# An attention block on one NeuronCore: query and key split in PSUM by TensorE, bias rows as three bf16 rows, sums turned once a batch

## The chip, the cores and the metric

The kernel runs on one NeuronCore of a Trainium2 chip; the other seven are not used. The metric is the device time of one execution in microseconds, the median over runs. Engines: TensorE (PE) multiplies into PSUM, VectorE (DVE), ScalarE (ACT) and GpSimd (POOL) compute, SyncE (SP) issues all DMAs. In this kernel only VectorE and ScalarE read PSUM.

## The reference, cut to what matters

```python
def _layernorm(t, gamma, beta):                      # over the last axis
    return (t - mean) * rsqrt(var + 1e-05) * gamma + beta
xn = (x - mean) / sqrt(var + 1e-05)                  # x is (32, 256, 128), f32
qkv = (xn @ Wqkv.T + bqkv).reshape(B, N, 3, H, D).transpose(2, 0, 3, 1, 4)   # H = 16, D = 8
q = _layernorm(q, q_gamma, q_beta)
k = _layernorm(k, k_gamma, k_beta)
aw = softmax(einsum('bhnd,bhmd->bhnm', q, k) / sqrt(D))
kth = top_k(aw, 12)[0][..., -1:]                     # topk = int(256 * 0.05)
aws = aw * (aw >= kth)
aws = aws / (aws.sum(-1, keepdims=True) + 1e-08)
o_s = einsum('bhnm,bhmd->bhnd', aws, v)
qf, kf = softmax(q), softmax(k)                      # over the 8 channels of a head
kv = einsum('bhnd,bhne->bhde', kf, v)
z = einsum('bhnd,bhd->bhn', qf, kf.sum(axis=2))
o_l = einsum('bhnd,bhde->bhne', qf, kv) / (z[..., None] + 1e-06)
a = sigmoid(alpha)                                   # one per head
o = a * o_s + (1.0 - a) * o_l
attn = o @ Wproj.T + bproj
idx = argmax(log_softmax(logits) + gumbel(u))        # one of 8 operators
y = x + attn + xn @ W[idx] + b[idx]
```

## The kernel before, in words

The 32 batches are 32 iterations `it`, unrolled by four in a hardware loop, with some iterations written out at either end. An iteration is a pass over eight *slots* `u_`, one for each *unit*; a unit is two heads, and for each of them two tiles of 128 queries by 256 keys, four tiles (`TILES`) in all. Each engine runs its own queue in the order in which `body` is written for it, and waits only on semaphores; nothing reorders the work across slots. Work is staged: in one slot each engine serves different units and even different batches.

The main line of unit g: TensorE multiplies its scores one slot ahead (`scores`, L797) into `score_ps`; VectorE takes the 8 largest of each tile (`top`, L503); GpSimd subtracts the maximum (`drop`, L363); ScalarE makes the exponentials `e` (L705) and `e8` (L710); one slot later VectorE strikes the 8 largest out (`rest`, L510) and takes the next 8 (`next`, L516), whose fourth is the threshold; GpSimd (three tiles, L389) and ScalarE (one tile, L718) mark what is `below` it; TensorE transposes `e` and adds -2^40 where `below` is set (`turn`, L814, L815, 16 matmuls a slot, into `turn_ps`); ScalarE's Relu makes `kept` of it (L666); every second slot TensorE multiplies four heads' `kept` by the values `v_aug`, which have a column of ones (`product`, L831, into the bank `pv_ps`), and ScalarE copies that to `oT` (L727).

Once a batch, around this:

- The sums of the four quads of `oT` are transposed back by TensorE (`sums`, L843, into `pv_ps`), for query tile 0 in slot 5 and for tile 1 in slot 7. VectorE adds `den` (L551), takes its reciprocal (L556) and writes `o_sparse` (L559), inside slots 5 and 7, behind its first two `rest`.
- The linear part: q and k of the next batch come out of the product L891 (slot 7, with a bias by a matmul of one row of ones with one row `b_row`, L892), pass ScalarE (`qk_sq`, `qk_raw`) and GpSimd (`qk_a`, `qk_b`, `qkn`), and `d_sub`; `q_exp` and `k_exp` are made by ScalarE in slot 4. In the next iteration TensorE multiplies `kv` (slot 1, L905, L907), transposes `q_exp` (slot 4, L943), ScalarE copies `qfT` (L733), TensorE multiplies both (slot 5, L869), and VectorE makes `lin_z` and `lin` (slot 5, L531, L534). 
- The exact split: `qkn` is transposed by TensorE (slot 3, L930) into the bank `work_ps`. ScalarE copies it to `qkT` in f32 (L686) and to bf16 `part[0]` (L689). GpSimd subtracts (`leave`, L352) to `residue`, ScalarE casts it to `part[1]` (slot 4, L738), once more for `part[2]` (slot 5). SyncE writes every part to DRAM in slots and reads them back as `q_slots` and `k_slots` for the scores of the next batch.
- The value product L880 with its bias L881 (slot 6), copied to `v_aug` (L693).
- The output: `o_sparse` and `lin` are transposed and added (slot 1, L862, L863), copied to `osT` (L672), and multiplied in slot 2, four products for each of two tiles (L918 the residual, L919 the chosen operator, L920 the bias, L921 the projection), copied in slot 3 to `out_sb` (L680) and stored.

All of these but the sums go through the one bank `work_ps`, one after the other, and every step waits for the copy of the last. TensorE's queue in a slot is: turn, product (even slots), sums (5 and 7), `early`, scores for the next unit, `late`.

## Time and profile before

| | |
|---|---|
| median of 3 runs | 1337.95 us (1335.01 to 1338.44) |
| the profiled execution | 1329.16 us, its span 1327.4 us |
| VectorE busy | 1212.3 us, 91% |
| ScalarE busy | 1135.2 us, 86% |
| GpSimd busy | 1092.6 us, 82% |
| TensorE matmul busy | 1051.5 us, 79% |
| DMA | 83.42 MB, 63 GB/s |

The times are those of one execution; "busy" leaves out semaphores, branches and DMA issue. Matmul records overlap, so a row's mean is a latency and not the distance from one to the next. A wait in the profile is idle time of an engine just before an instruction, with what released it. In rows of the timeline the first number is the start in us from the span's start, the second the duration.

### The profile page before, as it was taken

What the parts mean: (1) busy time and instruction counts of PE and PEld (TensorE: products, weight loads), DVE (VectorE), ACT (ScalarE), POOL (GpSimd) and SP (SyncE); (2) the same over time, 40 slices, a digit from 0 to 9 for tenths busy, and PEclk for the clock granted to TensorE, in tenths of its full rate; (3) what the DMA queues carried; (4) which work ended last, traced back from release to release, by engine and by line L of the source; (5) the groups of instructions that cost most, each with busy time, mean ns of one, the idle gap of its engine ahead of it and who ended that gap; (6) DMA issues with size and microseconds to landing.
All of it is one profiled execution on the core that took longest, in us unless ns stands there. A gap on an engine that the chain in (4) does not pass through costs nothing.

```text
span 1327.4 us, 39880 instructions
## 1 busy us (share of the span) xinstructions
PE 1051.5 (79%) x9156; PEld 718.5 (54%) x9156; DVE 1212.3 (91%) x4660; ACT 1135.2 (86%) x3946; POOL 1092.6 (82%) x1618
## 2 busy tenths in 40 slices
PE   3578887878787888887888887788878888887887
PEld 1345555555555555555555555555555555555555
DVE  5789999999899998999989999899989999999994
ACT  3588998998899897998888989788988889998984
POOL 4588888988789887889878889788888888889973
PEclk9979999998899998998989989889998889899998
DMA  2212221222222122221112222112221122221220
GB/s 57 68 45 73 76 77 43 60 65 65 79 77 70 36 64 65 77 77 52 56 53 75 77 77 60 46 53 77 77 79 34 58 65 77 76 77 37 61 58 13
DMA packets 165196, 83.42 MB, mean 63 GB/s; under 512 B 7747, under 2 KB 164933, under 8 KB 164934
## 3 DMA queue, kind: packets, MB, share of 16 engines
q1 hardware_dynamic: 164934, 80.54, 21.1%
q8 instruction: 89, 1.46, 0.5%
q14 instruction: 173, 1.42, 0.4%
HBM read 42.77 MB, written 37.75 MB: 61 GB/s over the span
## 4 chain that ended last, share of the span: by engine, by line
PE 34%; issue 21%; ACT 17%; POOL 13%; DVE 13%; DVEq 1%; POOLq 1%; ACTq 0%; DMA 0%; SPq 0%
PE turn_ps L814 9%; ACT e L705 9%; POOL below L389 8%; DVE rest L510 6%; PE turn_ps L815 4%; DVE top L503 4%; PE work_ps L892 3%; PE work_ps L891 3%; PE pv_ps L831 3%; DVE next L516 3%; PE score_ps L797 2%; PE pv_ps L843 2%; ACT xn L756 2%; PE work_ps L921 2%; ACT below L718 1%
## 5 line engine op out<-in xcount | busy, mean ns | idle before, releaser
L389 POOL TENSOR_SCALAR below<-e,next 128x256 bf16<-128x256 f32 x768 | 695.8, 921 | 0.0
L705 ACT ACTIVATE e<-score_ps,drop 128x256 f32<-128x256 f32 x1024 | 475.4, 492 | 76.1 <-POOL drop L363 75.6
L814 PE MATMUL turn_ps<-ident,e 128*128 128x128 f32 x2048 | 432.8, 304 | 29.1 <-issue 14.5
L510 DVE MATCH_REPLACE8 rest<-e 128x256 f32<-128x256 f32 x1024 | 413.1, 406 | 0.9 <-issue 0.9
L516 DVE MAX8 next<-rest 128x8 f32<-128x256 f32 x1024 | 410.5, 411 | 3.3 <-issue 1.8
L815 PE MATMUL turn_ps<-minus_huge,below 128*128 128x128 bf16 x2048 | 406.4, 234 | 0.0
L503 DVE MAX8 top<-score_ps 128x8 f32<-128x256 f32 x1024 | 360.2, 413 | 37.3 <-PE score_ps L797 19.8
L814 PEld LDWEIGHTS turn_ps<-ident,e 128*128 128x128 f32 x2048 | 314.4, 154 | 97.9 <-issue 31.5
L666 ACT ACTIVATE kept<-turn_ps 128x512 f32<-128x512 f32 x512 | 292.2, 624 | 67.0 <-PE turn_ps L815 62.6
L815 PEld LDWEIGHTS turn_ps<-minus_huge,below 128*128 128x128 bf16 x2048 | 234.7, 115 | 0.0
L705 ACT ACTIVATION_READ_ACCUMULATOR e<-score_ps,drop 128x1 f32 x1024 | 229.3, 224 | 0.0
L363 POOL TENSOR_TENSOR drop<-top 128x36 f32<-128x36 f32 x256 | 62.6, 245 | 133.8 <-DVE top L503 132.6
L831 PE MATMUL pv_ps<-kept,v_aug 128*32 128x256 f32 x2048 | 141.5, 395 | 1.1 <-ACT kept L666 0.7
L718 ACT ACTIVATE below<-e,next 128x256 bf16<-128x256 f32 x256 | 137.0, 535 | 0.2 <-DVE next L516 0.2
L797 PE MATMUL score_ps<-k_slots,q_slots 64*128 64x256 bf16 x1024 | 104.8, 283 | 12.0 <-ACT e L705 10.1
L510 DVE MATCH_VALUE_LOAD rest<-e 128x8 f32 x1024 | 73.2, 71 | 15.0 <-ACT e L710 13.0
L831 PEld LDWEIGHTS pv_ps<-kept,v_aug 128*32 128x32 f32 x2048 | 54.5, 111 | 46.2 <-issue 24.4
L843 PE MATMUL pv_ps<-ident,oT 128*128 128x128 f32 x256 | 49.6, 326 | 36.8 <-ACT oT L727 35.5
L797 PEld LDWEIGHTS score_ps<-k_slots,q_slots 64*128 64x128 bf16 x1024 | 30.7, 95 | 85.8 <-issue 76.6
L710 ACT ACTIVATE e<-drop 128x32 f32<-128x32 f32 x256 | 66.3, 259 | 0.0
L352 POOL TENSOR_TENSOR residue<-qkT,part 128x512 f32<-128x512 f32 x32 | 37.2, 1162 | 32.2 <-ACT part L689 31.9
L843 PEld LDWEIGHTS pv_ps<-ident,oT 128*128 128x128 f32 x256 | 33.7, 168 | 51.0 <-ACT oT L727 49.1
(141 smaller groups left out, 1529.7 us busy)
## 6 DMA issues: line engine op xcount, KB each, us to landing
part_slots<-part SPq DMA_DIRECT2D x128, 192.0 KB, 2.3
q_slots<-part_slots SPq DMA_DIRECT2D x64, 256.0 KB, 3.4
...
```

The costliest lines, as they stand in the source:

```text
L389: nc.gpsimd.tensor_scalar(below[:, r, t, :], e[:, r, t, :], next8[:, r, t, TOPK - 9:TOPK - 8], None, ALU.is_lt).then_inc(s["below_pool"], 1)
L503: nc.vector.max(top[:, q, t, 1:9], score_ps[:, q, t // 2, t % 2, :]).then_inc(s["top_ready"], 1)
L510: nc.vector.match_replace(rest[:, t, :], e8[:, (u_ - 1) % 2, t, :], e[:, (u_ - 1) % RING, t, :], REMOVED).then_inc(s["rest_ready"], 1)
L516: nc.vector.max(next8[:, (u_ - 1) % RING, t, :], rest[:, t, :]).then_inc(s["next_ready"], 1)
L666: nc.scalar.activation(kept[:, u_ % 4, hh], turn_ps[:, hh], ACT.Relu).then_inc(s["turn_copied"], 1)
L705: nc.scalar.activation(e[:, u_ % RING, t, :], score_ps[:, u_ % 2, t // 2, t % 2, :], ACT.Exp, bias=drop[:, u_ % 2, t, 0:1], accum_out=z[:, ...
L718: nc.scalar.activation(below[:, r, t, :], e[:, r, t, :], ACT.Relu, scale=-1.0, bias=next8[:, r, t, TOPK - 9:TOPK - 8]).then_inc(s["below_a ...
L797: last = mm(score_ps[:, v_ % 2, hh, nt, :], q_slots[rows, side, v_, nt * P:(nt + 1) * P], k_slots[rows, side, v_, :], start=True, stop=True)
L814: mm(dst, e[:, r, t, keys], ident[:], start=True, stop=False, is_transpose=True)
L815: last = mm(dst, below[:, r, t, keys], minus_huge[:], start=False, stop=True)
L831: last = mm(pv_ps[32 * j:32 * (j + 1), 0:N], v_aug[:, side, mc, 4 * q + j, :], kept[:, v_ % 4, j % 2, mc, :], start=(mc == 0), stop=(mc == ...
L843: last = nc.tensor.transpose(pv_ps[:, q * P:(q + 1) * P], oT[:, nxt, q, t * P:(t + 1) * P], ident[:])
```

## The change

1. **The split in PSUM.** `qkT`, `residue` and GpSimd's `leave` are gone. ScalarE casts `part[0]` from `work_ps`. TensorE then multiplies `part[p]` by `minus_one` (minus the identity, bf16) into the same bank without clearing it (`remainder`), for p = 0 late in slot 4 and for p = 1 early in slot 5; ScalarE casts `part[1]` and `part[2]` from `work_ps`, in the places where it cast them from `residue`. For that the four transposes of `qkn` are one accumulation group.
2. **Bias rows.** Each bias row is split at the start into three bf16 rows (`in_parts`, on VectorE), and a bias is added by one bf16 matmul with a contraction of three rows (`ones3`, `bias3`) in place of an f32 one with one row.
3. **The sums once a batch.** All eight transposes stand in slot 5, behind the scores. They use the matrix `gather` in place of the identity, which packs four heads' 9 used columns next to each other, so that the sums of both tiles fit the bank. VectorE's `den`, reciprocal and `o_sparse` run once, over both tiles, in slot 5.
4. **Other slots and banks.** `q_exp` is transposed early in slot 0 and copied there at the slot's end; the linear product moves from slot 5 to the end of slot 2, VectorE's `lin_z` and `lin` from slot 5 to slot 3. The transposes of `o_sparse` and `lin`, and the output's products, go to `pv_ps` in place of `work_ps`; the output moves from the end of slot 2 to slot 3, ahead of the scores.

TensorE, slot 5, before: the end of the turn, and what follows up to the scores of unit 6. `oT` are the copied sums, `part` the bf16 part.

```order
L815 MATMUL turn_ps<-minus_huge,below 128x128
L814 MATMUL turn_ps<-ident,e 128x128
L815 MATMUL turn_ps<-minus_huge,below 128x128
L843 MATMUL pv_ps<-ident,oT 128x128 x4
L869 MATMUL work_ps<-kv,qfT 128x144 x2
L73 ISA
L797 MATMUL score_ps<-k_slots,q_slots 128x256 x4
L805 REGISTER_ALU
```

And in the changed kernel, where `gather` stands for the identity:

```order
L834 MATMUL turn_ps<-minus_huge,below 128x128
L833 MATMUL turn_ps<-ident,e 128x128
L834 MATMUL turn_ps<-minus_huge,below 128x128
L871 REGISTER_ALU
L872 MATMUL work_ps<-part,minus_one 128x512
L73 ISA
L816 MATMUL score_ps<-k_slots,q_slots 128x256 x4
L865 MATMUL pv_ps<-gather,oT 128x128 x8
L824 REGISTER_ALU
```

The sums went from ahead of the scores to behind them, four became eight, the linear product left, and the remainder stands ahead of the scores.

TensorE, slot 7, before: the end of the turn, the sums of tile 1 and the query and key product of the batch after the next, up to the scores of the next batch's first unit.

```order
L814 MATMUL turn_ps<-ident,e 128x128
L815 MATMUL turn_ps<-minus_huge,below 128x128
L843 MATMUL pv_ps<-ident,oT 128x128 x4
L885 REGISTER_ALU
L891 MATMUL work_ps<-w_qk,xnT 128x256
L892 MATMUL work_ps<-b_row,ones_row 128x256
L891 MATMUL work_ps<-w_qk,xnT 128x256
L892 MATMUL work_ps<-b_row,ones_row 128x256
L789 REGISTER_ALU
L73 ISA
L797 MATMUL score_ps<-k_slots,q_slots 128x256 x4
```

In the changed kernel:

```order
L833 MATMUL turn_ps<-ident,e 128x128
L834 MATMUL turn_ps<-minus_huge,below 128x128
L924 REGISTER_ALU
L931 MATMUL work_ps<-w_qk,xnT 128x256
L932 MATMUL work_ps<-bias,ones 128x256
L931 MATMUL work_ps<-w_qk,xnT 128x256
L932 MATMUL work_ps<-bias,ones 128x256
L808 REGISTER_ALU
L73 ISA
L816 MATMUL score_ps<-k_slots,q_slots 128x256 x4
```

The sums are gone and the bias is taken from `bias` by `ones`, which are `bias3` and `ones3`.

TensorE, from the scores in slot 2 to the start of the next turn, before:

```order
L797 MATMUL score_ps<-k_slots,q_slots 128x256 x4
L915 REGISTER_ALU
L918 MATMUL work_ps<-x_res,ident 128x128
L919 MATMUL work_ps<-w_sel,xnT 128x128
L920 MATMUL work_ps<-b_out,ones_row 128x128
L921 MATMUL work_ps<-w_proj,osT 128x128
L918 MATMUL work_ps<-x_res,ident 128x128
L919 MATMUL work_ps<-w_sel,xnT 128x128
L920 MATMUL work_ps<-b_out,ones_row 128x128
L921 MATMUL work_ps<-w_proj,osT 128x128
L805 REGISTER_ALU
```

In the changed kernel, first the same place, and then slot 3 from the turn's end to the scores for unit 4:

```order
L816 MATMUL score_ps<-k_slots,q_slots 128x256 x4
L950 MATMUL work_ps<-kv,qfT 128x144 x2
L824 REGISTER_ALU
```

```order
L834 MATMUL turn_ps<-minus_huge,below 128x128
L901 REGISTER_ALU
L904 MATMUL pv_ps<-x_res,ident 128x128
L905 MATMUL pv_ps<-w_sel,xnT 128x128
L906 MATMUL pv_ps<-bias,ones 128x128
L907 MATMUL pv_ps<-w_proj,osT 128x128
L904 MATMUL pv_ps<-x_res,ident 128x128
L905 MATMUL pv_ps<-w_sel,xnT 128x128
L906 MATMUL pv_ps<-bias,ones 128x128
L907 MATMUL pv_ps<-w_proj,osT 128x128
L73 ISA
L816 MATMUL score_ps<-k_slots,q_slots 128x256 x4
```

The linear product stands where the output stood, and the output stands between the turn of slot 3 and the scores, in the bank `pv_ps`.

The diff, cut (left out: GpSimd's setup of the constants `minus_one`, `gather` and `ones3`, buffers and loads that go from one partition to three, and waits that follow from the moves):

```diff
-if u_ == 4 and exists(it + 1):
-    leave(it, 0)
-if u_ == 5 and exists(it + 1):
-    leave(it, 1)
...
+def in_parts(row, cols):
+
+    p0, p1 = bias_part[:, 0, cols], bias_part[:, 1, cols]
+    r1, r2, total = bias_rest[:, 0, cols], bias_rest[:, 1, cols], bias_sum[:, cols]
+    own = [ident[0:PARTS, p:p + 1] for p in range(PARTS)]
+    setup(nc.vector.tensor_copy(p0, row))
+    setup(nc.vector.tensor_tensor(r1, row, p0, ALU.subtract))
+    setup(nc.vector.tensor_copy(p1, r1))
+    setup(nc.vector.tensor_tensor(r2, r1, p1, ALU.subtract))
+    setup(nc.vector.tensor_scalar(total, p0, own[0], None, ALU.mult))
+    setup(nc.vector.scalar_tensor_tensor(out=total, in0=p1, scalar=own[1], in1=total, op0=ALU.mult,
+                                         op1=ALU.add))
+    return nc.vector.scalar_tensor_tensor(out=bias3[:, cols], in0=r2, scalar=own[2], in1=total,
+                                          op0=ALU.mult, op1=ALU.add)
...
-if u_ == 5 and 3 <= k <= 5 and exists(it):
+if u_ == 3 and k in (1, 3) and exists(it):
     w = work_ps[:, 0:NT * H * VA].rearrange("p (t h e) -> p t h e", t=NT, e=VA)
-    if k == 3:
+    if k == 1:
...
-if u_ in (5, 7) and 1 <= k <= 4 and exists(it - 1):
-    t = (u_ - 5) // 2
-    w = pv_ps[:].rearrange("p (h e) -> p h e", e=VW)
-    n = 2 * (NT * (it - 1) + t)
+if u_ == 5 and 1 <= k <= 4 and exists(it - 1):
+    w = pv_ps[:, 0:NT * H * VA].rearrange("p (g e) -> p g e", e=VA)
+    n = 2 * (it - 1)
     if k == 1:
-        dve.wait_ge(s["w_turn"], NT * (it - 1) + t + 1)
...
 if u_ == 4 and exists(it + 1):
     act.wait_ge(s["w_qkT"], it + 2)
-    wait(act, s["residue_ready"], 2 * (it + 1))
-    nc.scalar.copy(qkT[:], work_ps[:].rearrange("p (a n) -> p a n", a=2)).then_inc(
-        s["qkT_copied"], 1)
     wait(act, s["slots_written"], 16 * 2 * PARTS * (it + 1))
     nc.scalar.copy(part[:, 0], work_ps[:].rearrange("p (a n) -> p a n", a=2)).then_inc(
         s["part_ready"], 1)
...
-if u_ == 4 and exists(it):
+if u_ == 0 and exists(it):
     act.wait_ge(s["w_qfT"], it + 1)
+    wait(act, s["w_lin"], it)
     nc.scalar.copy(qfT[:], work_ps[:, 0:N]).then_inc(s["qfT_copied"], 1)
 if u_ in (4, 5) and exists(it + 1):
     p = u_ - 3
-    act.wait_ge(s["residue_ready"], 2 * (it + 1) + p)
-    nc.scalar.copy(part[:, p], residue[:, p - 1]).then_inc(s["part_ready"], 1)
+    act.wait_ge(s["w_rest"], 2 * (it + 1) + p)
+    nc.scalar.copy(part[:, p], work_ps[:].rearrange("p (a n) -> p a n", a=2)).then_inc(
+        s["part_ready"], 1)
...
+def sums():
+
+    pe.wait_ge(s["pv_copied"], QUADS * it)
+    for t in range(NT):
+        for q in range(QUADS):
+            at = (t * QUADS + q) * 4 * VA
+            last = nc.tensor.transpose(pv_ps[:, at:at + P], oT[:, nxt, q, t * P:(t + 1) * P], gather[:])
...
+def remainder(p):
+
+    pe.wait_ge(s["part_ready"], PARTS * (it + 1) + p + 1)
+    mm(work_ps[:], minus_one[:], part[:, p].rearrange("p a n -> p (a n)"), start=False,
+       stop=True, skip_group_check=True).then_inc(s["w_rest"], 1)
...
+    if u_ == 0 and exists(it):
+
+        pe.wait_ge(s["dexp_ready"], 2 * it + 1)
         if exists(it + 1):
             pe.wait_ge(s["raw_ready"], it + 2)
...
+if u_ == 3 and exists(it - 2):
+
+    pe.wait_ge(s["osT_copied"], it - 1)
+    pe.wait_ge(s["pv_copied"], QUADS * it - 1 if exists(it - 1) else QUADS * B)
+    pe.wait_ge(s["setup_v"], 7)
+    pe.wait_ge(s["res_loaded"], 16 * (it - 1))
     for t in range(NT):
-        last = mm(work_ps[:, t * H * VA:(t + 1) * H * VA], qfT[:, t * P:(t + 1) * P],
-                  kv[:].rearrange("p h e -> p (h e)"), start=True, stop=True)
-    last.then_inc(s["w_lin"], 1)
+        dst = pv_ps[:, t * C:(t + 1) * C]
+        mm(dst, ident[:], x_res[:, t, :], start=True, stop=False)
+        mm(dst, xnT[:, (xr - 2) % XRING, t * P:(t + 1) * P], w_sel[:], start=False, stop=False)
+        mm(dst, ones3[:], bias3[:, 3 * C:4 * C], start=False, stop=False)
+        last = mm(dst, osT[:, t * P:(t + 1) * P], w_proj[:], start=False, stop=True)
+    last.then_inc(s["w_out"], 1)
+if u_ == 5 and exists(it + 1):
+
+    remainder(1)
...
+    pe.wait_ge(s["part_ready"], PARTS * (it + 2))
     for t in range(NT):
         dst = work_ps[:, t * C:(t + 1) * C]
         mm(dst, xnT[:, (xr + 1) % XRING, t * P:(t + 1) * P], w_v[:], start=True, stop=False)
-        last = mm(dst, ones_row[:], b_row[:, 2 * C:3 * C], start=False, stop=True)
+        last = mm(dst, ones3[:], bias3[:, 2 * C:3 * C], start=False, stop=True)
...
-if u_ == 2 and exists(it - 2):
...
+if u_ == 2 and exists(it):
...
+        last = mm(work_ps[:, t * H * VA:(t + 1) * H * VA], qfT[:, t * P:(t + 1) * P],
+                  kv[:].rearrange("p h e -> p (h e)"), start=True, stop=True)
+    last.then_inc(s["w_lin"], 1)
 if u_ == 3 and exists(it + 1):
...
+    wait(pe, s["lin_ready"], it + 1)
...
+if u_ == 4 and exists(it + 1):
+
+    remainder(0)
...
-if u_ in (5, 7) and exists(it - 1):
-    sums(u_)
 early(u_)
 if exists(it if u_ < UNITS - 1 else it + 1):
     scores(u_)
+if u_ == 5 and exists(it - 1):
+    sums()
 late(u_)
```

## Rows read from the trace of the kernel before

**Rows 1.** The page, busy time of each engine, share of the span, instructions.

```profile
PE 1051.5 (79%) x9156; PEld 718.5 (54%) x9156; DVE 1212.3 (91%) x4660; ACT 1135.2 (86%) x3946; POOL 1092.6 (82%) x1618
```

**Rows 2.** Line 524, once a batch: durations, first and last start in us.

```profile
L524 DVE TENSOR_TENSOR kv<-work_ps,own_head x32: 288/295/298, 49.9 to 1279.1; 128x144 f32<-128x144 f32 x32
```

**Rows 3.** VectorE's waits, 85 to 1240 us: us in total, times, longest.

```profile
DVE den L551 <- PE pv_ps L843: 25.5, 42, 1.0
DVE top L503 <- issue: 16.5, 5, 3.7
DVE rest L510 <- ACT e L710: 10.5, 17, 0.9
DVE top L503 <- PE score_ps L797: 7.7, 17, 0.7
```

**Rows 4.** VectorE by line: busy us, mean ns | idle before, releaser.

```profile
L559 DVE TENSOR_TENSOR o_sparse<-pv_ps,den 128x128 f32<-128x128 f32 x64 | 17.2, 269 | 0.1
...
L556 DVE RECIPROCAL den<-den 128x16 f32<-128x16 f32 x64 | 14.9, 233 | 0.1
...
L534 DVE TENSOR_TENSOR lin<-work_ps,lin_z 128x256 f32<-128x256 f32 x32 | 12.9, 403 | 0.0
L531 DVE RECIPROCAL lin_z<-work_ps 128x32 f32<-128x32 f32 x32 | 11.0, 345 | 0.0
L551 DVE SCALAR_TENSOR_TENSOR den<-z,pv_ps 128x16 f32<-128x16 f32 x64 | 10.7, 167 | 36.0 <-PE pv_ps L843 35.7
```

**Rows 5.** Timeline, slots 4 and 5 of one batch, from four engines.

```profile
650.70 1.40 DVE L503 MAX8 top<-score_ps 128x8 f32<-128x256 f32 x4
...
652.31 0.63 ACT L686 COPY qkT<-work_ps 128x512 f32<-128x512 f32 x1
652.77 0.65 ACT L689 CAST part<-work_ps 128x512 bf16<-128x512 f32 x1
653.31 0.50 ACT L705 ACTIVATE e<-score_ps,drop 128x256 f32<-128x256 f32 x1
...
655.63 0.40 ACT L727 COPY oT<-pv_ps 128x256 f32<-128x256 f32 x1
...
656.09 0.66 PE L843 MATMUL pv_ps<-ident,oT 128*128 128x128 f32 x4 [0.74 <-ACT oT L727]
656.58 0.66 PE L869 MATMUL work_ps<-kv,qfT 128*128 128x144 f32 x4
657.17 0.40 PE L797 MATMUL score_ps<-k_slots,q_slots 64*128 64x256 bf16 x4
...
657.01 0.16 DVE L551 SCALAR_TENSOR_TENSOR den<-z,pv_ps 128x16 f32<-128x16 f32 x1
657.08 0.42 DVE L516 MAX8 next<-rest 128x8 f32<-128x256 f32 x1
```

**Rows 6.** Timeline, slots 2 and 3 of the same batch.

```profile
644.07 0.48 PE L918 MATMUL work_ps<-x_res,ident 128*128 128x128 f32 x2 [1.54 <-issue]
...
646.40 0.49 PE L921 MATMUL work_ps<-w_proj,osT 128*128 128x128 f32 x2
646.41 0.38 ACT L727 COPY oT<-pv_ps 128x256 f32<-128x256 f32 x1
...
648.78 0.37 ACT L680 COPY out_sb<-work_ps 128x256 f32<-128x256 f32 x1
```

**Rows 7.** By line, TensorE's f32 bias and GpSimd's subtraction, as in Rows 4.

```profile
L892 PE MATMUL work_ps<-b_row,ones_row 1*128 1x256 f32 x128 | 48.1, 457 | 0.0
...
L352 POOL TENSOR_TENSOR residue<-qkT,part 128x512 f32<-128x512 f32 x32 | 37.2, 1162 | 32.2 <-ACT part L689 31.9
```

**Rows 8.** TensorE in two turns, slots 5 and 7: us, busy (x), granted clock, DMA.

```profile
653.77:655.35 1.58, 1.58 (x18) 1.00 0.57 166
664.55:667.33 2.78, 2.78 (x18) 0.50 0.54 160
```

**Rows 9.** Timeline, VectorE's first maxima.

```profile
40.33 1.76 DVE L503 MAX8 top<-score_ps 128x8 f32<-128x256 f32 x5 [8.77 <-PE score_ps L797]
```

166 lines of the change are left out of this document (74 added, 92 removed).

## The prediction

> **What bounds the kernel now.** I read the busy shares first. VectorE leads with 91%, ScalarE, GpSimd and TensorE follow at 86, 82 and 79% [rows 1]: four engines that are all nearly full, so the question is which of them sets the pace and how often it stands still. One batch is 1229.2 / 31 = 39.65 us, from the first and last start of an operation that runs once a batch [rows 2]. In the unit loop VectorE has nearly no gap: its waits between 85 and 1240 us, which are 29.1 batches, add up to 43.7 us in the three lines that the change can touch, and 16.5 us in five long "issue" gaps of over 3 us, one at each turn of the hardware loop [rows 3]. The last have no engine behind them, so I leave them as they are. So VectorE sets the pace, and a batch is some 37.6 us of its own work, 0.57 us of loop turns and 43.7 / 29.1 = 1.50 us of waits for others: 25.5 us for the turned sums (`den` <- `pv_ps`), 10.5 us for the exponentials of the unit before (`rest` <- `e`), 7.7 us for scores [rows 3]. Whatever the change does on the other engines counts only through these waits, through VectorE's own instructions, or through a new wait on VectorE.
>
> **Part by part, per batch.** Slot u is pass u of the unit loop.
>
> *VectorE's own work.* Two sets of `den`, reciprocal and `o_sparse` (167 + 233 + 269 ns) become one with twice the elements. The nearest rows of that size are the reciprocal of 32 elements, 345 ns, and the product over 256, 403 ns; `den` of 32 elements I put at 180 ns, 167 plus the little that 16 elements add [rows 4]. That is 1.34 us against 0.93 us by durations, 0.4 us less. But these instructions overlap their neighbours: `den` starts at 657.01 and the MAX8 behind it at 657.08, where `den` lasts 0.16 us [rows 5]. An instruction thus costs some 0.08 us less than its duration, and three fewer of them save 0.41 - 0.24 = 0.17 us, which I take; the bounds are 0.1 and 0.4.
>
> *The sums of slot 7.* The wait of slot 7 (up to 1.0 us [rows 3]) has no instruction left to wait. Four transposes leave TensorE's queue there, and the query and key product loses its f32 bias matmuls, 457 ns each and two per 256 columns [rows 7], for one bf16 pass over the same columns. 128 columns of bf16 with their load take about 0.1 us (the turn's 16 matmuls, half of them bf16, in 1.58 us [rows 8]), so 256 take 0.1 to 0.2 us. The scores for the next batch stand behind that product, so they come over 1 us earlier, and the wait for scores (7.7 us, the longest 0.7) should go too.
>
> *The linear part and the output.* The linear part's product moves from slot 5 to slot 2, the output's four products per tile from slot 2 to slot 3, ahead of the scores for unit 4. Until now TensorE spends 644.07 to 646.89 on the output, and only then turns unit -1, which ScalarE needs before the exponentials of slot 3 [rows 6]. Now two small products stand there. The output must wait for ScalarE's copy of `pv_ps` (646.41 + 0.38 = 646.8 [rows 6]). It took 2.8 us; with bf16 bias it takes 2.2, so it ends at 649.0, and `out_sb`, which was copied at 648.78, is copied at 649.1: ScalarE's exponentials of slot 3 start 0.4 us later in a quiet batch. In a batch where the turn of slot 3 ran slowly they start earlier than now. VectorE's two `lin` instructions (345 + 403 ns, some 0.6 us after overlap) go from slot 5 to slot 3, ahead of the point where `rest` waits for `e`. Both together should remove most of the 10.5 us. I take all of it; if the cover fails, it costs 0.36 us a batch.
>
> *The split.* GpSimd loses two subtractions of 1.16 us [rows 7], ScalarE the copy `qkT` (it holds the queue 652.77 - 652.31 = 0.46 us [rows 5]). GpSimd's gain lies beside other work: its next job is to wait for VectorE's maxima. TensorE gains two matmuls of 512 bf16 columns, 0.2 to 0.4 us each by the turn's 0.1 us per 128. What matters is the order: `remainder(1)` stands ahead of the scores in slot 5 and waits for ScalarE's cast of the second part; behind it are queued the scores, and now the sums. Who waits for the sums is VectorE.
>
> *The new wait in slot 5.* All eight transposes now stand behind `remainder(1)` and the scores. In a quiet batch [rows 5]: VectorE starts the maxima of slot 4 at 650.70; behind GpSimd's `drop`, whose queue up to there is unchanged, ScalarE's exponentials start at 653.31 (the `qkT` copy gone gives 0.46 back, the later `out_sb` takes 0.4), the copy `oT` runs from 655.63 to 656.03, and before, the four transposes start at 656.09 and VectorE takes `den` at 657.01 without waiting. Now: `oT` at 656.1; the cast of the second part, so far a copy of 0.6 us like `qkT`, to 656.7; `remainder(1)` to 657.0; four score matmuls, 0.35 of their 0.40 [rows 5], to 657.3; eight transposes at 656.58 - 656.09 = 0.49 us for four, and 0.2 of latency, to 658.5. VectorE, moved 0.6 back by `lin`, asks at 657.6. It waits **0.9 us** in every batch, against nothing in this batch's slot 5 and up to 1.0 in slot 7 until now. The cause is a chain, not TensorE's load.
>
> *The clock.* On that chain TensorE idles some 1.4 us between the turn of slot 5 (653.77 to 655.35 [rows 8]) and `remainder(1)`. The trace shows both clocks on the same 16 matmuls: 1.00 granted, 1.58 us, behind a stretch that was nearly full; 0.50 granted, 2.78 us, in slot 7, where TensorE had idled before the transposes of `xn` [rows 8]. At half clock the eight transposes take 0.98 x 2.78 / 1.58 = 1.7 us, and with the two steps ahead of them the wait becomes 1.9 us. I put in about a third of the batches, 0.35 us on average, as the idle time in slot 2 (1.54 us [rows 6]) is also followed by half clock only in some. The same slow spells in slots 2 and 3 now fall on the turn and the output that lead to `out_sb`; 0.3 us a batch, between 0 and 0.8.
>
> The Trainium skill ("TensorE: Matmul & The Clock Gate", Part 4) says that a transpose on TensorE does not count as work for the clock gate, so that full clock does not engage for it. Half of the turn's matmuls are transposes and it ran at 1.00, so the trace speaks against the plain form of the rule. By the rule the slot 5 chain, mostly transposes, would sit at half clock in each batch: that is the slower rival below.
>
> *Edges.* Setup splits three bias rows on VectorE, seven small instructions each, and `stage_gate` stands ahead of `d_max`. But VectorE then waits 8.77 us for the first scores [rows 9], so at most some 2 us reach them through `d_max`; the end loses f32 bias matmuls. I take +0.5 us for both, from -1 to +3.
>
> **Sum.** Gone: 1.50 us of waits and 0.17 of work. New: 0.9 + 0.35 + 0.3 = 1.55. Net -0.12 us, by 31 batches -4 us; with the edges -3. The profiled execution took 1329.16 us (span 1327.4), the median of the three runs is 1337.95: the profiled one was 0.7% quicker, and I apply the difference of -3 us to the median: **1335 us**. A measurement of this kernel can tell some 0.3% (4 us) from no change, so the forecast itself lies inside that.
>
> **Rivals.** *The clock stays full* (0.23). TensorE's idle times in slots 2 and 6 shrink, since work moves into them. Then only the 0.9 us remain: 0.9 - 1.67 = -0.77, by 31 -24 us: 1314. For it: the turns of the trace run mostly at 1.00. Against: the change takes more than 1 us of matmul work away and leaves a longer idle time in slot 5.
> *Half clock on the slot 5 chain in every batch* (0.24). 1.9 + 0.3 - 1.67 = +0.53, by 31 +16 us: 1354; with the slow output too (0.8 for 0.3) 1370. It decides from a new wait of 1.67 us a batch on: more than that, and the change loses. For it: the slow turn of slot 7 also stands behind an idle TensorE. Against: the turn of slot 5 just ahead is dense. The rule of the Trainium skill quoted above would give this rival's time.
>
> *The exponentials stay late* (0.06). If the output at its new place holds ScalarE as long as the old one did, the 0.36 us stay: -3 + 11 = +8, 1346.
> The forecast has 0.47, itself from 1326 to 1344, with half of it over 4 us below the median and a tenth over 4 us above it.
>
> **Numbers.** 80% range: 1312 to 1358, from the full clock's 1314 to a little beyond half clock's 1354. Faster by over 0.3%: 0.23 of the forecast and 0.23 of the full clock, 0.46. Within 0.3%: 0.19 and 0.02 of the late exponentials, 0.21. Slower: 0.05 + 0.24 + 0.04 = 0.33.
>
> **What would show it.** `den` is waited for once a batch and for 0.9 to 1.9 us, as VectorE's largest wait; none in slot 7; the waits for scores and for `e` are near zero; `out_sb` is copied before 649.2 in the frame above; the granted clock of the stretch from `remainder(1)` to the last sum tells the rivals apart. VectorE waiting for loaded slots, or for `lin`'s product in slot 3, would make the whole account wrong.

## The result, and the profile after

| | before | after |
|---|---|---|
| median | 1336.48 us (1329.57 to 1338.44, 4 runs) | 1299.38 us (1298.57 to 1301.66, 4 runs) |
| the profiled execution | 1329.16 us, span 1327.4 | 1299.64 us, span 1297.9 |

The changed kernel is faster: ratio 0.9734, 95% interval 0.9696 to 0.9773. The forecast was 1335 with a range of 1312 to 1358; the result lies 13 us below the range. Of the rivals, the full clock (1314) comes nearest.

The page after, busy times, then the row of the granted clock in 40 slices; and the row of the once-a-batch operation, which answers to [rows 1, 2]:

```profile
PE 987.9 (76%) x9028; PEld 664.9 (51%) x9028; DVE 1204.0 (93%) x4585; ACT 1112.9 (86%) x3914; POOL 1025.0 (79%) x1560
...
PEclk9999999998899998999989999889999899999988
```

```profile
L545 DVE TENSOR_TENSOR kv<-work_ps,own_head x32: 287/295/306, 52.7 to 1251.9; 128x144 f32<-128x144 f32 x32
```

A batch takes 1199.2 / 31 = 38.68 us against 39.65: 30.0 us of the span. The start is 2.8 us longer (49.9 to 52.7), the end 2.3 shorter (48.3 to 46.0).

VectorE's waits after, 85 to 1240 us, as in [rows 3]:

```profile
DVE den L571 <- PE pv_ps L865: 28.7, 30, 1.9
DVE top L524 <- issue: 17.2, 5, 4.0
DVE top L524 <- PE score_ps L816: 6.2, 7, 2.3
DVE rest L531 <- ACT e L727: 0.8, 3, 0.3
```

The wait for `e` is all but gone; of the one for scores seven are left in place of 17, and four of them, 5.4 of the 6.2 us, stand behind a turn of the hardware loop; `den` waits once in each batch. Slot 5 of one batch, timeline of ScalarE, TensorE and VectorE, then the stretch of the chain in the windows view (busy us of TensorE, its weight loads, VectorE, ScalarE, GpSimd; then the granted clock, DMA share, GB/s):

```profile
759.54 0.44 ACT L744 COPY oT<-pv_ps 128x256 f32<-128x256 f32 x1
759.79 0.67 ACT L756 CAST part<-work_ps 128x512 bf16<-128x512 f32 x1
...
760.52 0.39 PE L872 MATMUL work_ps<-part,minus_one 128*128 128x512 bf16 x1 [1.23 <-ACT part L756]
760.84 0.39 PE L816 MATMUL score_ps<-k_slots,q_slots 64*128 64x256 bf16 x4
761.17 1.10 PE L865 MATMUL pv_ps<-gather,oT 128*128 128x128 f32 x8
...
762.30 0.19 DVE L571 SCALAR_TENSOR_TENSOR den<-z,pv_ps 128x32 f32<-128x32 f32 x1 [0.94 <-PE pv_ps L865]
```

```profile
760.50:762.25 1.75, 1.73 (x15) 1.28 (x16) 0.86 (x5) 1.75 (x6) 1.47 (x5) 1.00 0.45 127
```

This is the predicted chain, copy, cast, remainder, scores, eight transposes, with the predicted wait. It runs at 1.00, the 2.4 GHz level, and so it does in all 30 batches from the `den` at 104.6 us to the one at 1227.8: from the start of the remainder to the end of the last sum it takes 1.74 us each time.

### The profile page after: what moved, and what is told of

Same layout as the page of the kernel before. It is cut to its first block, busy times and chain, and to the rows that moved or that the text cites. A ratio compares the mean times of both kernels' runs of the same rounds, so it can differ in the third digit from the quotient of the medians.

```text
span 1297.9 us, 39296 instructions
## 1 busy us (share of the span) xinstructions
PE 987.9 (76%) x9028; PEld 664.9 (51%) x9028; DVE 1204.0 (93%) x4585; ACT 1112.9 (86%) x3914; POOL 1025.0 (79%) x1560
## 4 chain that ended last, share of the span: by engine, by line
DVE 32%; issue 25%; PE 19%; ACT 15%; POOL 4%; DVEq 4%; SPq 0%; ACTq 0%; DMA 0%; POOLq 0%
DVE rest L531 12%; DVE top L524 11%; ACT e L722 8%; DVE next L537 4%; PE turn_ps L833 4%; DVEq L73 3%; POOL below L389 3%; PE pv_ps L865 2%; ACT kept L686 2%; PE pv_ps L907 2%; PE turn_ps L834 2%; PE pv_ps L904 2%; PE work_ps L950 2%; ACT part L756 1%; PE score_ps L816 1%
## 5 line engine op out<-in xcount | busy, mean ns | idle before, releaser
L833 PE MATMUL turn_ps<-ident,e 128*128 128x128 f32 x2048 | 411.8, 294 | 26.3 <-issue 23.0
L834 PE MATMUL turn_ps<-minus_huge,below 128*128 128x128 bf16 x2048 | 388.4, 228 | 0.0
L833 PEld LDWEIGHTS turn_ps<-ident,e 128*128 128x128 f32 x2048 | 302.9, 148 | 85.8 <-issue 43.6
L834 PEld LDWEIGHTS turn_ps<-minus_huge,below 128*128 128x128 bf16 x2048 | 227.2, 111 | 0.4 <-issue 0.2
L854 PE MATMUL pv_ps<-kept,v_aug 128*32 128x256 f32 x2048 | 144.5, 401 | 22.4 <-DVE o_sparse L579 21.9
L854 PEld LDWEIGHTS pv_ps<-kept,v_aug 128*32 128x32 f32 x2048 | 57.9, 113 | 70.3 <-issue 52.0
L931 PE MATMUL work_ps<-w_qk,xnT 128*128 128x256 f32 x128 | 46.8, 448 | 45.2 <-ACT xnT L779 45.2
L872 PE MATMUL work_ps<-part,minus_one 128*128 128x512 bf16 x64 | 25.8, 404 | 58.6 <-ACT part L756 38.4
L950 PE MATMUL work_ps<-kv,qfT 128*128 128x144 f32 x128 | 25.2, 322 | 42.5 <-DVE kv L545 42.2
```

The costliest lines, as they stand in the source:

```text
L833: mm(dst, e[:, r, t, keys], ident[:], start=True, stop=False, is_transpose=True)
L834: last = mm(dst, below[:, r, t, keys], minus_huge[:], start=False, stop=True)
L854: last = mm(pv_ps[32 * j:32 * (j + 1), 0:N], v_aug[:, side, mc, 4 * q + j, :], kept[:, v_ % 4, j % 2, mc, :], start=(mc == 0), stop=(mc == ...
```

## Experiments

Each ratio is to the kernel before on the same chip, whose medians were 1332.9 to 1336.8 us; gains against it are told in the text from these. Differences between two variants are differences of their medians; where the two ran on different chips, the ratios can give another figure, by up to 8 us, and where that matters both stand in the text. The last two columns come from one profiled execution each. Granted half clock (1.2 GHz) was added up over 85 to 1210 us in steps of a quarter microsecond; "part" numbers are those of the change.

| kernel | median us | ratio, 95% interval | half clock us | us per batch |
|---|---|---|---|---|
| before | 1336.5 | 1 | 167 | 39.65 |
| changed (1+2+3+4) | 1299.4 | 0.973 (0.970 to 0.977) | 96 | 38.68 |
| b_bias_bf16 (2) | 1302.6 | 0.977 (0.974 to 0.979) | 184 | 38.66 |
| b_bias_qk | 1322.4 | 0.990 (0.986 to 0.994) | 214 | 39.37 |
| b_bias_v | 1346.6 | 1.010 (1.006 to 1.013) | 195 | 39.87 |
| b_bias_out | 1316.0 | 0.986 (0.982 to 0.990) | 132 | 38.95 |
| b_fill6 | 1323.2 | 0.991 (0.988 to 0.994) | 123 | 39.53 |
| b_bias_fill6 | 1289.1 | 0.963 (0.956 to 0.970) | 99 | 38.26 |
| b_leave_small | 1307.2 | 0.980 (0.972 to 0.987) | 181 | 39.01 |
| p4 (4) | 1344.8 | 1.008 (1.004 to 1.012) | 181 | 40.13 |
| p24 (2+4) | 1322.6 | 0.992 (0.989 to 0.996) | 157 | 39.37 |
| p14 (1+4) | 1296.1 | 0.974 (0.970 to 0.977) | 82 | 38.31 |
| a_sums_twice (1+2+4) | 1269.2 | 0.948 (0.941 to 0.955) | 82 | 37.67 |
| a_bias_f32 (1+3+4) | 1315.3 | 0.987 (0.984 to 0.989) | 92 | 38.98 |
| a_split_pool (2+3+4) | 1314.4 | 0.986 (0.981 to 0.990) | 160 | 38.94 |
| a_split_fill6 | 1306.3 | 0.975 (0.968 to 0.983) | 109 | 38.99 |
| a_den_late | 1269.8 | 0.953 (0.950 to 0.956) | 64 | 37.61 |
| a_sums_first | 1262.9 | 0.943 (0.936 to 0.950) | 93 | 37.66 |
| t_pool_load | 1286.2 | 0.962 (0.958 to 0.966) | 102 | 38.28 |
| d_loop8 | 1257.7 | 0.944 (0.939 to 0.948) | 55 | 37.37 |

### The sums, part 3: den later, sums ahead, sums in two halves

```diff
--- a_den_late, against the changed kernel (VectorE, slot 5: den, reciprocal, o_sparse)
-                    if u_ == 5 and 1 <= k <= 4 and exists(it - 1):
+                    if u_ == 5 and k >= 4 and exists(it - 1):
...
-                        if k == 1:
+                        if k == 4:
...
-                        if k == 2:
+                        if k == 5:
...
-                        if k == 4:
+                        if k == 6:
...
+                    extra(u_, 6)
```

> The changed kernel with VectorE's den, reciprocal and o_sparse later in slot 5: behind the second next, behind the third, and behind the last. The sums are then ready when den is reached, so its wait of 0.94 us in each of 31 batches should be gone: -29 us, about 1271, if the wait was only one of order (theory 1). Against it (theory 2): o_sparse is finished some 2 us later, TensorE's product of slot 6 waits for it, and the value product and the scores behind it come later; if that is more than the slack of the scores, the wait comes back as one for scores in slot 7 and the gain is below 10 us.

```diff
--- a_sums_first, against the changed kernel (TensorE)
+                    if u_ == 5 and exists(it - 1):
+                        sums()
                     early(u_)
                     if exists(it if u_ < UNITS - 1 else it + 1):
                         scores(u_)
-                    if u_ == 5 and exists(it - 1):
-                        sums()
```

> The changed kernel with the eight transposes of the sums in slot 5 ahead of remainder(1) and of the scores. By the prediction's chain the wait of den is 1.9 us from the copy of oT less remainder, cast and scores: cast 0.6, remainder 0.3, scores 0.35 leave it, 1.25 us in all, so den waits for 0 in place of 0.94 us: -29 us if nothing else is late. The scores of slot 6 come 1 us later; if VectorE has less slack there than that, some of it comes back (theory: slack of the scores is 1.5 us or more, so none does).

```diff
--- a_sums_twice, against the changed kernel (TensorE, and den, reciprocal, o_sparse once for each half)
+                    if u_ in (5, 7) and exists(it - 1):
+                        sums(u_)
                     early(u_)
...
-                    if u_ == 5 and exists(it - 1):
-                        sums()
```

> The changed kernel with the sums in two halves again, each ahead of what else TensorE has in slots 5 and 7, and with den, reciprocal and o_sparse once for each. By the prediction's terms: VectorE's own work +0.17 us a batch, the wait in slot 5 0.94 -> 0.1 to 0.5, a wait in slot 7 of at most 0.3 where the turn runs at full clock: -0.9 + 0.17 + 0.4, about -10 us against the changed kernel, 1290. If the idle time in slot 6 grows with the sums out of its way (theory A), the clock in slot 7 falls and it is 0 to +15 us.

The three give 1269.8, 1262.9 and 1269.2 us, 30, 37 and 30 below the changed kernel (27, 41 and 34 by the ratios). VectorE's waits of a_den_late and then of a_sums_twice, 85 to 1210 us:

```profile
DVE top L524 <- issue: 18.3, 5, 4.0
DVE top L524 <- PE score_ps L817: 8.6, 10, 2.1
DVE den L571 <- PE pv_ps L866: 0.2, 1, 0.2
```

```profile
DVE top L524 <- issue: 18.2, 5, 4.3
DVE top L524 <- PE score_ps L818: 6.5, 5, 2.2
DVE den L573 <- PE pv_ps L869: 0.4, 2, 0.2
```

The wait of 0.94 us was one of order, and it was the whole loss: 0.94 x 31 = 29 us. The slack behind `o_sparse` and behind the scores was there. The third run says more: with the sums in two halves, as before the change, no wait is left in slot 5 or in slot 7. So part 3 was not needed to remove the wait of slot 7, since the others do it, and in the order in which the change placed the sums it cost 30 us. It is the order that costs and not the merging: a_sums_first has the sums merged too and is no slower than a_sums_twice (its runs span 1259.6 to 1267.9 us, those of a_sums_twice 1265.5 to 1270.1). For a_sums_twice I had expected 10.

### The bias rows, part 2

```diff
--- b_bias_bf16, against the kernel before (and in_parts with its tiles; the output and the value product alike)
-                            last = mm(dst, ones_row[:], b_row[:, 0:2 * C], start=False, stop=True)
+                            last = mm(dst, ones3[:], bias3[:, 0:2 * C], start=False, stop=True)
```

> The kernel before with the bias part of the change alone: three bf16 rows in place of one f32 row for all three biases. TensorE loses about 0.5 us of work in each of slots 2, 6 and 7. Theory A (clock): the idle time in slot 6 grows from 1.6 to some 2.1 us and the half clock behind it stays, so the wait for the sums in slot 7 stays near 25 us; only the wait for scores (7.7 us) goes: -2 to -8 us. Theory B (queue): less work stands ahead of the scores of slot 7, -8 to -15 us.

b_bias_qk, b_bias_v and b_bias_out make that edit at one place each.

> The kernel before with only the bias of the query and key product (slot 7, two matmuls of 256 columns) as three bf16 rows. The run with all three biases gained 31 us, 0.99 us a batch, of which the waits of VectorE explain some 0.8. Theory Q (the scores of slot 7 stand behind this product): this one alone gives 15 us or more, and the waits for scores go. Theory O (what counts is the output in slot 2, which delays the turn and ScalarE's exponentials of slot 3): this one alone gives 3 to 10 us.

> The kernel before with only the bias of the value product (slot 6, two matmuls of 128 columns) as bf16 rows. Both theories: TensorE idles 1.64 us behind this product, so half a microsecond less ahead of that idle time is worth little, 0 to -5 us; and if the idle time sets the clock of slot 7 (theory A), the longer idle time makes the slow turn as frequent as before or more.

> The kernel before with only the bias of the output (slot 2, two matmuls of 128 columns) as bf16 rows. Theory O: the turn of slot 3 and the exponentials behind it start 0.5 us earlier, the waits of VectorE for e (9.9 us between 85 and 1210 us) fall below 4, and the kernel is 8 to 20 us faster. Theory Q: 0 to -6 us.

```diff
--- a_bias_f32, against the changed kernel (the three places)
-                            last = mm(dst, ones3[:], bias3[:, 0:2 * C], start=False, stop=True)
+                            last = mm(dst, ones_row[:], b_row[0:1, 0:2 * C], start=False, stop=True)
```

> The changed kernel with the bias rows added by f32 matmuls of one row again (the split rows are still made at the start, but not used). If the bias rows carry a part of the gain through TensorE's queue (theory B), it is 8 to 15 us slower than the changed kernel. If the gain lies in the clock and the sums (theory A), it is 0 to 6 us slower: the scores of slot 7 come 0.5 us later, and VectorE had nothing to wait for there.

All three places together give 31 us, more than either theory allowed, and nearly as much as the whole change: the changed kernel is only 3 us faster than b_bias_bf16. The output's bias alone gives 20 and takes the wait for `e` away, as theory O had it; the query and key product's gives 13, where theory Q wanted 15 or more; the value product's alone costs 11, a sign that no theory had. The three add up to 22 us, not 31. Each of these kernels, with the bias rows split at its start, also starts later: `kv` first runs at 55.0 to 55.7 us in place of 49.9, so some 6 of the 11 us of b_bias_v are the start's, and 7 (0.22 x 31) come from its batches. VectorE's waits for `e` and scores, 85 to 1210 us, in b_bias_out, and then TensorE's idle time ahead of the transposes of `xn` (slot 6) in b_bias_v, 200 to 1200 us:

```profile
DVE top L530 <- PE score_ps L824: 4.8, 8, 3.2
DVE rest L537 <- ACT e L737: 1.7, 8, 0.3
```

```profile
PE work_ps L979 <- issue: 53.7, 25, 2.2
```

Before, that idle time was 1.63 us a batch. Made 0.5 longer, by half a microsecond less work ahead of it, it goes with more half clock (195 us for 167), and VectorE's wait for scores doubled, from 7.5 to 15.9 us. That the clock is what made it slower is argued, not shown: b_bias_qk has 214 us of half clock and is 13 us faster. Inside the changed kernel the bias rows are worth 16 us: without them `den` waits for 41.0 us in place of 27.3 (85 to 1210 us). Beside parts 1 and 4 they are worth 27 us (p14 against a_sums_twice; 35 by the ratios).

### The clock: work put into TensorE's idle time

```diff
--- b_fill6, against the kernel before (TensorE, behind the scores of slot 6)
+FILL = 14
...
+                    if u_ != 6:
+                        last.then_inc(s["pv_ready"], 1)
+
+                def fill():
+
+                    for i in range(FILL):
+                        last = mm(pv_ps[:, 2 * P:3 * P], minus_huge[:], minus_huge[:], start=True, stop=True)
                     last.then_inc(s["pv_ready"], 1)
...
+                    if u_ == 6 and exists(it):
+                        fill()
```

The edit moves one thing more than was expected of it: in slot 6 ScalarE's copy of the product (`oT`) is now released behind the filler, and no longer behind the product.

> The kernel before with one addition: in slot 6, behind the scores, TensorE issues 14 bf16 matmuls of 128 columns into columns of the bank pv_ps that nobody reads (about 1.4 us at full clock), where it otherwise stood idle for 1.6 us ahead of the transposes of xn. Nothing else moves. Theory A (clock): the kernel before loses time because the idle time in slot 6 is followed by half clock in the turn, the sums and the query and key product of slot 7. Then those 16 matmuls take 1.6 in place of 2.8 us, VectorE's wait for the sums (25.5 us between 85 and 1240 us) falls below 10 us, and the kernel runs 12 to 25 us faster than the kernel before, though TensorE does more work. Theory B (queue): slot 7 was late because of what stands in TensorE's queue (sums, two f32 bias matmuls); then the added work gains nothing, -3 to +5 us.

> The kernel before with all three biases as bf16 rows (31 us faster than before by itself) and, behind the scores of slot 6, 18 bf16 matmuls of 128 columns into unread columns of pv_ps, about 1.2 us. Theory A (the idle time of TensorE in slot 6 sets the clock of slot 7; by itself the filler gave 10 us to the kernel before, and the bias of the value product, which makes that idle time longer, cost 11 us): granted half clock falls from 184 us between 85 and 1210 us to under 110, and the kernel is 8 to 18 us faster than with the biases alone, 1285 to 1295. Theory C (the clock in slot 7 costs nothing once the queue is shorter): within 4 us of 1302.6.

```diff
--- a_split_fill6 is a_split_pool with 20 such matmuls
+FILL = 20
...
+                    for i in range(FILL):
+                        last = mm(pv_ps[:, 3 * P:4 * P], minus_huge[:], minus_huge[:], start=True, stop=True)
```

> The changed kernel with the split on GpSimd again (15 us slower than the changed kernel by itself, with an idle time of 2.4 us of TensorE in slot 6, since the sums come early and the product of slot 6 no longer waits for o_sparse, and 160 us at half clock in place of 95) and 20 bf16 matmuls of 128 columns in that idle time. Theory A: the clock is the cause of those 15 us; then the waits for scores (20.8 us) fall below 10 and it comes back to within 5 us of the changed kernel or below it, 1290 to 1305. Theory G (GpSimd's two subtractions of 1.16 us a batch are the cause): it stays at 1310 to 1318.

In b_fill6, slot 6, the filler, the idle time that is left, and the turn of slot 7, which now runs at 1.00 in 1.58 us, where [rows 8] show 0.50 and 2.78:

```profile
665.26 0.95 PE L841 MATMUL pv_ps<-minus_huge 128*128 128x128 bf16 x14
667.00 0.41 PE L961 MATMUL work_ps<-ident,xn 128*128 128x128 f32 x2 [0.78 <-issue]
```

```profile
667.30:668.88 1.58, 1.58 (x17) 1.27 (x16) 1.57 (x5) 1.58 (x9) 1.36 (x2) 1.00 0.10 28
```

Useless work on TensorE makes the kernel faster: by 10 us in the kernel before (its interval is 8 to 16), less than the 12 to 25 of theory A, and by 13 us with the bf16 bias rows (18 by the ratios). Theory A also had the wait for the sums below 10 us in b_fill6, and there it missed: it fell from 24.8 to 15.5, while those for `e` and for scores rose from 9.9 and 7.5 to 13.2 and 9.5 (85 to 1210 us). With the bf16 rows the theory did hold, in time and in half clock (184 to 99 us). The wait for the sums fell from 20.5 to this, 85 to 1210 us:

```profile
DVE den L579 <- PE pv_ps L878: 8.9, 29, 0.4
```

So the clock is a real cause, worth some 10 to 13 us at this place. It isn't the main one: b_bias_bf16 has more half clock than the kernel before and is 31 us faster. a_split_fill6 does not settle the matter. Half clock fell from 160 to 109 us, and the medians give 8 us (14 by the ratios) of the 15 of theory A, but the batch of the profiled executions is no shorter (38.99 us for 38.94), and the waits for scores, which theory A had below 10 us, rose from 20.8 to this. Part of what holds them is a transfer, in TensorE's wait below; both 85 to 1210 us:

```profile
DVE top L541 <- PE score_ps L835: 23.9, 19, 3.4
PE score_ps L835 <- DMA k_slots<-part_slots: 9.0, 6, 3.1
```

### The split, part 1, and the other slots, part 4

```diff
--- a_split_pool, against the changed kernel
+                    if u_ == 4 and exists(it + 1):
+                        leave(it, 0)
+                    if u_ == 5 and exists(it + 1):
+                        leave(it, 1)
...
-                        remainder(1)
...
-                        remainder(0)
```

> The changed kernel with the split of query and key on GpSimd again (the qkT copy, two subtractions, parts 1 and 2 cast from residue), without the two matmuls by minus_one; all else as changed. If, as the prediction has it, GpSimd's release lies beside other work and TensorE's remainder(1) is in the chain to the sums, this is 3 us faster to 6 us slower than the changed kernel, and den waits about 0.6 us for the sums in place of 0.94. If GpSimd (82% busy before) bounds anything, it is 10 us or more slower.

p24 has the same edit against a_sums_twice, p14 that of a_bias_f32, p4 both.

> Parts 2 and 4: the changed kernel with the split on GpSimd and the sums in two halves. Against parts 1, 2 and 4 (1269 us) it tells what the split in PSUM gives: 15 us inside the changed kernel. In the changed kernel the last part is cast 16.9 us behind kv, with the split on GpSimd 18.5 us, and the slots of the next batch are loaded behind that. Theory D (the transfers): 8 to 20 us slower than 1269, with waits of TensorE for k_slots and of VectorE for the first scores of a batch. Theory N (as predicted, worth nothing): within 5 us.

> Parts 1 and 4: the changed kernel with f32 bias rows and the sums in two halves. Against parts 1, 2 and 4 (1269 us) it tells what the bias rows give when the rest is there: alone they gave 31 us, inside the changed kernel 16. If their work on TensorE is what counts, it is 25 to 31 us slower than 1269; if the slots' order has taken that over, 10 to 16.

> Part 4 of the change alone (linear part and output in other slots and banks): the changed kernel with f32 bias rows, the split on GpSimd and the sums in two halves ahead of TensorE's other work. Parts 1, 2 and 4 together give 1269 us, part 2 alone 1305 us of 1336. If part 4 carries the 36 us that are left (theory P4: VectorE's lin, 0.6 us, goes ahead of the point where it asks for the sums, ScalarE's qfT copy leaves slot 4, so slot 5's sums are in time), this is 15 to 30 us faster than the kernel before. If the split carries them (theory P1: ScalarE's qkT copy goes and the parts reach the slots earlier), 0 to 10 us.

Part 4 alone is 0.8% slower than the kernel before, and theory P4 falls. Beside part 2 it costs 20 us (1302.6 to 1322.6). The split is worth 15 us inside the changed kernel and 53 us beside parts 2 and 4 (1322.6 to 1269.2; 60 by the ratios), far beyond theory D, whose transfers TensorE waits for only once there, for 1.4 us; beside part 4 it gives 49. The prediction gave it nothing. All these gains are counted on top of part 4: against part 2 alone, parts 1 and 4 together give 33 us, and the split without part 4 was not run. Inside the changed kernel it works both ways: with the split on GpSimd the wait for the sums is shorter (13.6 us for 27.3), as one expects with remainder(1) out of the chain, and the one for scores longer (20.8 for 6.2). VectorE's waits in a_split_pool, then all of them in p24, 85 to 1210 us:

```profile
DVE top L540 <- PE score_ps L834: 20.8, 14, 3.7
DVE den L587 <- PE pv_ps L883: 13.6, 21, 1.3
```

```profile
DVE top L540 <- issue: 18.1, 5, 4.1
DVE den L589 <- PE pv_ps L887: 15.2, 35, 1.2
DVE rest L547 <- ACT e L748: 13.4, 46, 0.4
DVE top L540 <- PE score_ps L836: 11.8, 10, 3.3
```

GpSimd in the kernel before, from the `drop` of slot 0 to that of slot 7 in the batch of [rows 5], with VectorE's maxima of slot 5. Where `drop` has no bracket, GpSimd came to it late, and the maxima had waited for it:

```profile
634.10 0.25 POOL L363 TENSOR_TENSOR drop<-top 128x36 f32<-128x36 f32 x1 [3.00 <-DVE top L503]
...
638.54 0.24 POOL L363 TENSOR_TENSOR drop<-top 128x36 f32<-128x36 f32 x1
...
643.72 0.24 POOL L363 TENSOR_TENSOR drop<-top 128x36 f32<-128x36 f32 x1
...
653.02 0.25 POOL L363 TENSOR_TENSOR drop<-top 128x36 f32<-128x36 f32 x1
653.50 1.16 POOL L352 TENSOR_TENSOR residue<-qkT,part 128x512 f32<-128x512 f32 x1 [0.23 <-ACT part L689]
654.64 2.72 POOL L389 TENSOR_SCALAR below<-e,next 128x256 bf16<-128x256 f32 x3
...
654.90 1.40 DVE L503 MAX8 top<-score_ps 128x8 f32<-128x256 f32 x4
...
658.87 0.24 POOL L363 TENSOR_TENSOR drop<-top 128x36 f32<-128x36 f32 x1
659.08 1.17 POOL L352 TENSOR_TENSOR residue<-residue,part 128x512 f32<-128x512 f32 x1
660.22 2.74 POOL L389 TENSOR_SCALAR below<-e,next 128x256 bf16<-128x256 f32 x3
662.93 0.25 POOL L363 TENSOR_TENSOR drop<-top 128x36 f32<-128x36 f32 x1
...
666.36 0.24 POOL L363 TENSOR_TENSOR drop<-top 128x36 f32<-128x36 f32 x1 [0.49 <-DVE top L503]
```

From 634.1 to 666.1 GpSimd never waits for a maximum. Its 82% is a full queue over six slots of eight and idle time in the other two, and not in this batch alone: over 200 to 1200 us, 25 batches, it waits for maxima 51 times, two of eight `drop`s a batch, against 85 times in 26 batches of the changed kernel:

```profile
POOL drop L363 <- DVE top L503: 91.8, 51, 6.2
POOL drop L367 <- DVE top L524: 154.3, 85, 4.8
```

VectorE has the maxima of slot 5 at 654.90 + 1.40 = 656.3; their `drop` comes at 658.87, and ScalarE's exponentials, the copy `oT` behind them and the sums hang on it. In the changed kernel, slots 5 to 7, GpSimd waits for VectorE:

```profile
799.13 0.25 POOL L367 TENSOR_TENSOR drop<-top 128x36 f32<-128x36 f32 x1
799.36 2.74 POOL L389 TENSOR_SCALAR below<-e,next 128x256 bf16<-128x256 f32 x3
804.92 0.25 POOL L367 TENSOR_TENSOR drop<-top 128x36 f32<-128x36 f32 x1 [2.83 <-DVE top L524]
...
809.33 0.25 POOL L367 TENSOR_TENSOR drop<-top 128x36 f32<-128x36 f32 x1 [1.47 <-DVE top L524]
```

Two runs take GpSimd's time by itself.

```diff
--- b_leave_small, against the kernel before
+            nc.gpsimd.memset(residue[:], 0.0).then_inc(s["zeroed"], 1)
...
-                src = qkT[:] if p == 0 else residue[:, 0]
-                nc.gpsimd.tensor_tensor(residue[:, p], src, part[:, p], ALU.subtract).then_inc(s["residue_ready"], 1)
+                src = qkT[:, :, 0:8] if p == 0 else residue[:, 0, :, 0:8]
+                nc.gpsimd.tensor_tensor(residue[:, p, :, 0:8], src, part[:, p, :, 0:8], ALU.subtract).then_inc(s["residue_ready"], 1)
```

> The kernel before with GpSimd's two subtractions of the split made over 8 of 256 columns of each half only (leave, L352; the rest of residue stays zero, so parts 1 and 2 of query and key are left out for the other columns, and its time is read for GpSimd's work alone). ScalarE's qkT copy, the casts, the transfers, the sums and the f32 bias rows all stay. Theory G: GpSimd works without a pause from the qkn step of slot 3 to slot 6, its drop comes late there, so the exponentials and all behind them do, and some 2 us less of its work a batch is worth 20 us or more (part 1 gave 53 us beside parts 2 and 4). Theory S (ScalarE's qkT copy and TensorE's place): GpSimd's work is worth nothing, within 5 us of the kernel before.

```diff
--- t_pool_load, against a_sums_twice (GpSimd, where leave stood)
+                    if u_ in (4, 5) and exists(it + 1):
...
+                        nc.gpsimd.tensor_tensor(load_c[:, u_ - 4], load_a[:], load_b[:], ALU.subtract).then_inc(
+                            s["load_done"], 1)
```

> Parts 1, 2 and 4 of the change (1269 us), with two subtractions of 128x512 on GpSimd put in at the places where it made the split before (slots 4 and 5), from constants into a tile that nobody reads, waiting for no other engine. Nothing else moves. Theory G: GpSimd's drop is late again, VectorE waits for e and for the sums, and this loses most of the 53 us that lie between 1269 and the kernel with the split on GpSimd (1323): 1300 to 1325. Theory S: within 5 us of 1269.

Taken away in the kernel before, 1.9 us of GpSimd's 2.3 us a batch (two subtractions of 0.22 us for two of 1.16) give 30 us by the medians, as theory G had it. The figure is loose: the runs spread from 1302 to 1318, the interval is 18 to 37 us, and the profiled executions differ by 21. Put back beside parts 1, 2 and 4 the 2.3 us cost 17 us, above theory S and below theory G. The wait that came back there, then the waits of b_leave_small for `e` and the sums (before: 9.9 and 24.8), 85 to 1210 us:

```profile
DVE den L583 <- PE pv_ps L879: 14.0, 29, 0.9
```

```profile
DVE rest L512 <- ACT e L712: 14.6, 22, 0.9
DVE den L553 <- PE pv_ps L845: 8.7, 27, 0.5
```

So GpSimd's time is a cause, worth some 17 to 30 us, and what it holds up are the sums. It is not the cause of the wait for `e`, which rose when its work was taken away. The other 36 of the 53 us stay open. Three things, at least, differ between p24 and t_pool_load: the real subtractions also wait for ScalarE's casts, 22.7 us over 200 to 1200 us in p24 and none in t_pool_load; ScalarE makes the `qkT` copy; and half clock is 157 us in place of 102. No run separates them.

### The loop turns

```diff
--- d_loop8, against a_den_late
-            with engine.Fori(first, last - 3, XRING) as i:
-                for j in range(XRING):
-                    body(i + j, j % 2, j)
+            with engine.Fori(first, last - 7, 2 * XRING) as i:
+                for j in range(2 * XRING):
+                    body(i + j, j % 2, j % XRING)
```

> The changed kernel with den, reciprocal and o_sparse late in slot 5 (1270 us), and the hardware loop unrolled by eight batches in place of four: three passes in place of six, so two turns in place of five. Each turn costs VectorE 3.2 to 4.0 us of idle time with nothing behind it, and another 0.5 to 2.1 us of waiting for scores behind it. Three turns fewer: -12 to -18 us, 1252 to 1258. If the gap is not the turn's but that of loading the code ahead, it stays, 1265 to 1270.

1257.7 us, the fastest here, 12 us below a_den_late and at the near end of what was expected. The turns' gap fell from 18.3 us in five to 7.3 in two, 85 to 1210 us; a turn costs 3.7 us with twice the code in the loop's body, so the gap goes by the number of turns, not by the length of the code:

```profile
DVE top L524 <- PE score_ps L817: 11.6, 13, 1.5
DVE top L524 <- issue: 7.3, 2, 4.0
```

## Why the prediction was wrong, step by step

- **VectorE sets the pace**: half true. It had the most work, but GpSimd fed ScalarE late through six of eight slots, and 16 of the 24.8 us for sums went with 1.9 us a batch of GpSimd's work (b_leave_small). The wait for `e` was another matter: the output's f32 bias on TensorE (9.9 to 1.7 us in b_bias_out). I read the releaser of each wait and not what had held the releaser.
- **Waits that go, 1.50 us a batch**: right for `e` and the sums of slot 7. Of the 7.7 us for scores 6.2 are left, in seven waits in place of 17, longest 2.3.
- **The new wait, 0.9 us**: right. 28.7 / 30 = 0.96 us.
- **The clock, +0.35 and +0.3 us**: this step failed, sign and all. It put half clock on the chain of slot 5 in a third of the batches. The chain ran at 1.00 in 30 of 30, behind an idle time of TensorE of 1.23 us in the batch shown, the waits show no addition, and the clock rose: half clock fell from 167 to 96 us. By itself the error is 0.65 x 31 = 20 us; with the scores' 6 us against it, and smaller gaps, all waits together missed 17 us (idle time of VectorE a batch, period less busy time: 39.65 - 37.21 = 2.44 before, 38.68 - 36.74 = 1.94 after, -0.50 against the +0.05 of the sum). I looked for the idle time that the change makes in slot 5 and took for granted that the one in slot 6 stays. It shrank from 1.63 to 0.2 us, since the product of slot 6 now starts later (it waits 0.7 us for `o_sparse`) and fills the time until `xn` can be turned.
- **VectorE's own work, -0.17 us**: too small. Busy time over 200 to 1200 us was 938.50 us before, 949.88 after; times the batch, 37.21 and 36.74 us, -0.47. Merging itself gives little: a_sums_twice and a_sums_first (972.34) differ by 36.70 - 36.62 = 0.08. The rest goes with the waits: a_sums_twice has the instructions of the kernel before, once the start is over, and 0.5 us less busy time. Counting every idle gap of VectorE over 200 to 1200 us, short ones too, there are 5.8 a batch before, 0.9 in a_sums_twice, and in p4, the busiest at 37.32 us, 7.3; over all 20 profiles it comes to about 0.1 us of busy time a gap. My reading, which no run tests by itself, is that a stalled instruction also loses its overlap with the one ahead. (0.47 - 0.17) x 31 = 9 us.
- **The split, nothing for GpSimd**: wrong, "its next job is to wait for VectorE's maxima" is contradicted by the rows above. It did little harm to this sum, since the waits that it fed were counted as gone already. But it hid that parts 1, 2 and 4 alone remove the wait for sums in both slots, and so that part 3's 0.9 us bought nothing.
- **The bias rows**: priced only as time ahead of the scores and of the output; alone they are worth 31 us.
- **Edges, +0.5**: right, 2.8 - 2.3 = 0.5 us.
- **The base**: the spans differ by 29.5 us, the medians by 37.1. I applied the profile's difference to the median; but the profiled execution before (1329.16) was 7 us under its median, the one after (1299.64) at it. That is another 8 us, and the median before came out 1.5 lower.

Together: 17 + 9 + 8 + 1.5 = 35.5, and 1335 - 35.5 = 1299.5. Of the rivals, half clock on the chain of slot 5 is refuted by the 30 chains at 1.00. (Its price was a little low by its own terms: 0.9, 0.7 for the transposes and 0.5 for remainder and scores make 2.1, not 1.9.) The rule that would have led to it (the Trainium skill, "TensorE: Matmul & The Clock Gate", Part 4: a transpose does not engage full clock) is not borne out here: eight transposes behind one matmul and the scores took 1.10 us at 1.00. The full clock's 1314 had the mechanism, but only half its reason, "idle times in slots 2 and 6 shrink, since work moves into them": the one ahead of the last product of slot 2 stays (34.1 us before, 33.2 after, over 200 to 1200 us), and the one of slot 6 shrinks because its work starts later. It also missed VectorE's own work and the base. That it came nearest is partly luck: the bias rows and the split, which it priced at little or nothing, are worth 16 and 15 us inside the changed kernel, and their worth reached the sum only because it had written off all the old waits.
